# Softplus of dt made for two channel blocks at once in a fused Mamba and mixture-of-experts layer; six row buffers for expert tiles in place of seven

## The reference

```python
x = x + attn(_layernorm(x))     # the Mamba block, with a residual of its own
x = x + moe(_layernorm(x))      # top 2 of 8 experts

# the Mamba block, after its own layer norm
u, z = jnp.split(xn @ W_in.T, 2, axis=-1)                # 512 channels each
u_c = silu(causal_conv_4_taps(u) + conv_b)
dt, Bm, Cm = jnp.split(u_c @ W_xp.T, [16, 32], axis=-1)
dt = softplus(dt @ W_dt.T + b_dt)                        # per token and channel
h = exp(dt * A) * h + dt * u * B                         # 16 states per channel, over 1024 tokens
y = (h * C).sum(state) + u * D
out = x + (y * silu(z)) @ W_out.T

# the experts
weights, which = top_k(x @ router_w + router_b, 2); weights = softmax(weights)
out[token] += weight * ((silu(rows @ gate_e) * (rows @ up_e)) @ down_e)
```

## Time and profile before

| | |
|---|---|
| median of 3 runs | 2355.94 us (2353.19 to 2358.41) |
| span of the profiled execution | 2343.2 us, so 12.7 us of the median lie around the span |
| busy, share of the span | POOL 84%, DVE 81%, PE 77%, ACT 77% |
| granted TensorE clock, mean | 0.884 of 2.4 GHz |
| DMA engines, mean | 158 GB/s |

### The profile page before, as it was taken

How to read it: one execution, slowest core, us unless ns; L and a number is a source line. 1 busy time by engine, 2 the same in 40 slices (tenths; PEclk the granted TensorE clock), 3 DMA queues, 4 the chain that set the end, 5 groups by cost and what they waited for, 6 DMA issues and landing times.

```text
span 2343.2 us, 32677 instructions
## 1 busy us (share of the span) xinstructions
PE 1793.1 (77%) x7694; PEld 922.2 (39%) x7694; DVE 1891.2 (81%) x2437; ACT 1808.0 (77%) x3753; POOL 1961.7 (84%) x1320
## 2 busy tenths in 40 slices
...
GB/s 57 136 90 135 109 134 115 121 170 179 172 159 198 174 192 171 165 184 172 175 158 199 174 197 174 159 176 175 175 157 201 176 193 166 181 259 221 71 51 33
DMA packets 217980, 369.35 MB, mean 158 GB/s; under 512 B 31040, under 2 KB 86592, under 8 KB 217664
## 3 DMA queue, kind: packets, MB, share of 16 engines
...
...
## 4 chain that ended last, share of the span: by engine, by line
POOL 31%; issue 25%; PE 14%; ACT 12%; DVE 10%; DMA 7%; POOLq 1%; DVEq 0%; ACTq 0%; SPq 0%
POOL arena L1326 11%; DMA out<-yt,xt 6%; DVE dA L1114 5%; POOL arena L1334 5%; PE ring L605 4%; POOL sorted_x L1364 4%; POOL out L1374 3%; POOL rst L1290 3%; ACT dA L977 2%; DVE arena L1114 2%; POOL arena L1344 2%; POOL arena L1349 2%; PE yps L699 2%; PE ring L613 1%; PE ring L625 1%
## 5 line engine op out<-in xcount | busy, mean ns | idle before, releaser
L1326 POOL TENSOR_TENSOR arena<-arena,b_bc 128x2048 f32<-128x2048 f32 x256 | 998.6, 3901 | 64.8 <-PE yps L699 64.5
L977 ACT ACTIVATE dA<-arena,a_s 128x512 f32<-128x512 f32 x1024 | 680.7, 684 | 120.9 <-DVE arena L1123 74.7
L1114 DVE TENSOR_TENSOR_SCAN dA<-dA,arena 128x512 f32<-128x512 f32 x384 | 454.7, 1214 | 175.2 <-ACT dA L977 108.8
L1114 DVE TENSOR_TENSOR_SCAN dA<-dA,carry,arena 128x512 f32<-128x512 f32 x384 | 477.6, 1275 | 66.6 <-POOL arena L1326 49.8
L699 PE MATMUL yps<-arena,const_s 128*32 128x512 f32 x2048 | 321.3, 704 | 84.1 <-POOL arena L1334 53.6
L1334 POOL TENSOR_TENSOR arena<-arena,c_bc 128x511 f32<-128x511 f32 (+1 forms) x256 | 335.6, 1311 | 28.0 <-DVE arena L1114 26.4
L1123 DVE TENSOR_TENSOR arena<-dA,c_bc 128x1024 f32<-128x1024 f32 x256 | 313.6, 1225 | 8.8
L1374 POOL DMA_INDIRECT out<-yt,xt x135 | 214.7, 1590 | 116.5 <-ACT yt L1018 84.5
L597 PE MATMUL ring<-arena 128*128 128x512 f32 x488 | 271.7, 684 | 52.9 <-ACT arena L881 24.5
L731 PEld LDWEIGHTS p_g<-xT,w_e 128*128 128x128 f32 x1680 | 218.8, 211 | 125.4 <-issue 125.4
L605 PE MATMUL ring<-arena 128*128 128x512 f32 x480 | 235.3, 635 | 33.7 <-ACT arena L881 12.1
...
## 6 DMA issues: line engine op xcount, KB each, us to landing
arena<-dt_d SPq DMA_DIRECT2D x512, 256.0 KB
w_e<-in_w_moe SPq DMA_DIRECT2D x105, 512.0 KB, 4.7
dt_d<-arena SPq DMA_DIRECT2D x128, 256.0 KB, 2.4
w_e<-in_w_moe SPq DMA_DIRECT2D x105, 256.0 KB
...
b_bc<-bc_d SPq DMA_DIRECT2D x256, 64.0 KB, 2.4
c_bc<-bc_d SPq DMA_DIRECT2D x256, 64.0 KB, 3.5
...
```

The lines of the kernel that those rows point to most:

```text
L977: act.activation(dA[:, j, :], rep_dt[:, c % 2, j, :], ACT.Exp, scale=a_s[:, n, j:j + 1]).then_inc(s_exp, 1)
L1114: return dve.tensor_tensor_scan(out_ap, dA[:, j, :], hs[:, u % 3, j, :], init, ALU.mult, ALU.add)
L1326: pool.tensor_tensor(hs[:, u % 3], rep_dtu[:, c % 2], b_bc[:, g, :].unsqueeze(1).to_broadcast([P, J, T]), ALU.mult).then_inc(s_dbu, 1)
```

## The change

Blocks go in groups. Batch 0 has the groups (0), (1), (2, 3); every other batch (0, 1), (2, 3). `E` and `L` and POOL's four steps work on a whole group, 1024 wide for two blocks; `D` stays one block at a time. So the four POOL steps and the four ACT steps occur 33 times (3 + 15 x 2) in place of 64. Their slots, of a batch other than 0, in the kernel before and in this one:

| step | before, blocks 0, 1, 2, 3 | now, groups (0, 1), (2, 3) |
|---|---|---|
| `round_off` | -9, -4, -1, 1 | -9, -1 |
| `less_lost` | -8, -3, 0, 2 | -8, 0 |
| `plus_relu` | -7, -2, 0, 4 | -7, 1 |
| `dtu` | -6, -2, 0, 4 | -6, 2 |
| `store_dt` (SP) | -4, -1, 1, 6 | -5, -5, 3, 3 |

The tables for PE and ACT follow; the core of the diff:

```diff
-NX, NY = 7, 2
+NX, NY = 6, 2
 MAKES = {...
-         ["D0"], (-9, 1): ["Z0"], ... (-6, 0): ["D1"], (-2, 0): ["D2"], (0, 4): ["D3"]
+         ["D0"], (-9, 0): ["D1"], (-9, 2): ["Z0"], ... (-2, 0): ["D2"], (-1, 0): ["D3"]
 TAKES = {...
-         (-9, 0): ["D0", "E0"], (-9, 3): ["Z0"], (-8, 0): ["L0"], ...
-         (-6, 1): ["D1"], (-5, 1): ["E1"], (-3, 0): ["L1"], (-1, 0): ["D2", "E2"],
-         (0, 1): ["L2"], (1, 3): ["D3", "E3"], (2, 2): ["L3"]
+         (-9, 0): ["D0"], (-9, 2): ["D1", "E0"], (-9, 4): ["Z0"], (-8, 0): ["L0"], ...
+         (-1, 0): ["D2"], (-1, 1): ["D3", "E2"], (0, 1): ["L2"]
+def groups(q):
+    return ((0, 1), (1, 1), (2, 2)) if q == 0 else ((0, 2), (2, 2))
+def columns(q, k):
+    c, n = groups(q)[k]
+    return slice(c % 2, c % 2 + n)
-        t_s = sb("t_s", [P, T])
+        t_s = sb("t_s", [P, 2, T])
-        past = sb("past", [P, LAST, NE + 2])
-        full = sb("full", [P, NE, NTH])
+        past_t = sb("past", [P, NE + 2, LAST])          # full now lies in past's memory
             def exp_abs(q, c):
-                act.wait_ge(s_ract, TAKEN[q, f"D{c}"])
-                act.activation(dtub[:, c % 2, :], dtub[:, c % 2, :], ACT.Exp, scale=-1.0).then_inc(s_e, 1)
+                act.wait_ge(s_ract, TAKEN[q, f"D{sum(groups(q)[k]) - 1}"])
+                act.activation(dtub[:, of, :], dtub[:, of, :], ACT.Exp, scale=-1.0).then_inc(s_e, 1)
...
-            def round_off(q, c):
-                pool.wait_ge(s_s, CC * q + c + 1)
-                pool.tensor_tensor(t_s[:], t_s[:], dtub[:, c % 2, :], ALU.add).then_inc(s_t, 1)
+            def round_off(q, k):
+                pool.wait_ge(s_s, done_groups(q, k))
+                pool.tensor_tensor(t_s[:, of], t_s[:, of], dtub[:, of, :], ALU.add).then_inc(s_t, 1)
```

More of the change, by code:

```diff
@@ L131, in pieces, with group_at, group_of, done_groups @@
     return [(q, c) for q in range(NQ) for c in range(CC) if s == UN * q + (at if q > 0 else first)[c]]
+def groups(q):
+    return ((0, 1), (1, 1), (2, 2)) if q == 0 else ((0, 2), (2, 2))
+def group_at(s, at, first):
+    return [(q, k) for q in range(NQ) for k in range(len(groups(q))) if s == UN * q + (at if q > 0 else first)[k]]
+def group_of(q, c):
+    return next(k for k, (first, n) in enumerate(groups(q)) if first <= c < first + n)
+def done_groups(q, k):
+    return sum(len(groups(p)) for p in range(q)) + k + 1
+def columns(q, k):
+    c, n = groups(q)[k]
+    return slice(c % 2, c % 2 + n)
 def ahead(s, n, second):
@@ L277, in mamba_moe @@
         step = sb("step", [P, NE + 2])
-        past = sb("past", [P, LAST, NE + 2])
-        full = sb("full", [P, NE, NTH])
+        past_t = sb("past", [P, NE + 2, LAST])
+        past = past_t[:, :, :].rearrange("p e k -> p k e")
+        full = past_t[:, 0:NE - 2].rearrange("p e k -> p (e k)")[:, 0:NE * NTH].rearrange("p (e h) -> p e h", h=NTH)
         tef = sb("tef", [P, LAST])
@@ L541, in _ @@
                 front = 0 <= q + 1 < NQ
-                for p, k in pieces(s, (-4, -1, 1, 6), (-10, -1, 3, 6)):
+                for p, k in pieces(s, (-5, -5, 3, 3), (-10, -1, 3, 3)):
                     store_dt(p, k)
@@ L902, in exp_abs @@
             def exp_abs(q, c):
[L903 to L910 removed]
+                k = group_of(q, c)
+                of, v = columns(q, k), done_groups(q, k)
+                act.wait_ge(s_ract, TAKEN[q, f"D{sum(groups(q)[k]) - 1}"])
+                act.activation(dtub[:, of, :], dtub[:, of, :], ACT.Exp, scale=-1.0).then_inc(s_e, 1)
+                act.wait_ge(s_e, v)
+                wait(act, s_sub, v - 1)
+                act.activation(t_s[:, of], dtub[:, of, :], ACT.Identity, bias=1.0).then_inc(s_one, 1)
+                act.wait_ge(s_one, v)
+                act.activation(t_s[:, of], t_s[:, of], ACT.Identity, bias=1.0, scale=-1.0).then_inc(s_s, 1)
             def log_one(q, c):
[L913 to L914 removed]
+                k = group_of(q, c)
+                of = columns(q, k)
+                act.wait_ge(s_t, done_groups(q, k))
+                act.activation(dtub[:, of, :], dtub[:, of, :], ACT.Ln, bias=1.0).then_inc(s_l, 1)
             def silu_u(q):
```

44 lines of the change are left out of this document (19 added, 25 removed), and 14 rows, old and new, of tables (MAKES, MAKES0, TAKES, TAKES0).

## The result

The changed kernel takes 2515 us (median of four, 2502 to 2518) where the kernel before takes 2355 (2351 to 2358, measured beside it): ratio 1.068, 95% interval 1.064 to 1.071. The forecast was 2461 with a range of 2385 to 2500: the direction was right, the size was not.

The account below looks back on a forecast made before the run. The prediction took POOL to set the pace in slots 7 to 11: 3.8 + 3.8 - 0.6 = 7.0 us a batch, slots 12 to 6 at 0. 15 x 7.0 = 105 on 2356 gave 2461 us, range 2385 to 2500.

Parts of the forecast that it names:

- Bound of slots 7 to 11: Slots 7 to 11: POOL is the tight engine, each microsecond put into it moves every later scan; loss 7.0 us a batch.
- parts 1 and 2: Slots 7 to 11: `round_off` waits 3.8 us for ACT's t; wider POOL pieces add 3.8, a wait for `place` saves 0.6.
- prices: POOL's 1024-wide pieces take 2.00 us, wide `plus_relu` 1.1 more than its 1.28; ACT's 1024 columns take 1.06.
- POOL sets the pace: Slots 7 to 11: POOL has 35.7 us with one 0.61 wait, while DVE sits idle 5.71 for the `drive` of unit 12.
- Part 3: Slots 7 and 8: `K0`, `place` and first scatter some 3 us later, no extra cost as POOL comes later still; floor 5.9.
- Part 4: Slots 12 to 6: POOL's and ACT's shifts net to 0 us a batch, bounds -5.1 to +2.
- 2.2 - 1.4 + 1.3: POOL's lateness: `drive` of unit 1 2.2 us later, slot 0 1.4 less work, slot 1 1.3 more.
- ACT's 6.4 us less in slots 1 and 2: ACT loses a take, three steps and a logarithm with its loads, which can shorten DVE's 3.37 wait at unit 6.
- Parts at nothing: Joined stores, block 2's reads, six `xt` buffers, the tail's loads and `full` in `past`'s memory: no cost.
- more is lost: Rival: POOL's delay in slots 15 to 3 isn't made up, or the tail waits for loads: 2491 and more; chance 0.08.
- The saving pays: Rival: 80 us of ACT's table loads and 22 us of POOL's fixed parts go: 2305 or 2334; chance 0.13.
- The lead is given back: Rival: slots 12 to 6 return 3 to 5 of the 7.0, through ACT's 6.4 us: 2386 to 2416; chance 0.15.

Follow-up runs that it names:

- e18: Kernel before with only ACT's work for block 1 moved up to slot 7 and `D1` ahead of `Z0`, all pieces 512 wide: 2425 us, ratio 1.031.
- e11: Changed kernel with the first pair's `round_off` one slot later, `less_lost` beside `plus_relu`: 2557 us, ratio 1.086.
- e12: Changed kernel with both edits, `K0` ahead of `Z0` and the first pair's `round_off` one slot later: 2513 us, ratio 1.068.
- e10: Changed kernel with `K0` put ahead of `Z0` in the ring: 2510 us, ratio 1.068.
- e15: Changed kernel with only blocks 0 and 1 paired; ACT's block 3 work in slot 15, POOL's pieces for blocks 2, 3 512 wide in old slots: 2450 us, 1.042.
- e14: Kernel before with only ACT's work and matmul for block 3 moved up to slot 15, all pieces 512 wide: 2397 us, ratio 1.018.
- e20: Changed kernel with the stores of blocks 1 and 3 in the slots of the kernel before: 2521 us, ratio 1.071.
- e1: Kernel before with six row buffers and nothing else: 2353 us, ratio 0.999.

## Why the prediction was wrong

**Bound of slots 7 to 11, parts 1 and 2, prices: right, one reason incomplete.** The forecast was 7.0 us a batch, measured 6.9. `round_off` waits 3.3 to 3.9 in slot 7 (3.8 forecast), the wide pieces take 2.00 and 2.35, the logarithm's loads are 33. But the two terms are not one wait and four longer pieces: ACT's joined block, with `D1` ahead of `Z0`, makes 4.4 (e18) and the wide pieces the other 2.5. So that the sum came out at 6.9 is in part luck. e11 and e12 show that the wait is not `round_off`'s own; it goes to whatever POOL wants next from ACT, directly or through DVE's `place`. "POOL sets the pace" was half of it: POOL and ACT set it together. DVE's wait at unit 12 came out at 7.6 in the mean (7.7 to 8.3 in most batches, 5.4 before) and not at 9 or more: of the stretch's 6.9 only 2.2 are that wait; DVE was busy for 3.8 more, 3.1 of that in one small instruction (last section), and waited 1.0 more at units 8 and 11. In e12 that instruction is short again, DVE waits at units 10 to 12 instead, and the stretch is as long.

**Part 3: right in direction.** I put `K0` 3 us later and hidden behind POOL. It is 4.3 to 4.5 later (medians of even and odd batches, 5.1 in batch 8) and about ties with POOL. That it costs nothing while `round_off` waits holds (e10), and that it takes the place of that wait holds too (e11: 4.19).

**Part 4: the step that failed.** It read "I take 0, since the two work on the same stretch in turn", with bounds from -5.1 to +2; measured is +4.6 (12 to 15: -0.6, 0 to 3: +2.9, 4 to 6: +2.2), above the upper bound. Two errors are in it. First, I netted POOL's lateness in slots 15 to 2 against its earliness from slot 4 on, "+0.6 by slot 5, with a peak of 3 at the drive of unit 4, where DVE waits already now". Its first term was right: `round_off` of slot 15 went 1.2 later (1.3 forecast). But the drive of unit 3 ended 3.2 later after unit 15's product than before (mean of 14 batches; by my terms 2.2 - 1.4 + 1.3 = 2.1), since I missed POOL's wait for the landing of an add, 2.77 in slot 1 of batch 8 and 1.7 in the mean. DVE's scan of unit 3 moved by the same 3.2 (4.84 of waiting for 1.09). The waits that DVE had at units 2 and 3 didn't cover it, because ACT's joined block had used them up: it had made DVE 2.4 late at unit 1 already. And being early later is worth nothing: POOL just waits longer for PE (120.3 us for 64.5, in slot 6 6.0 a batch for 2.3). Second, ACT's 6.4 us less in slots 1 and 2 was to shorten DVE's wait at unit 6; it did not: DVE's 2.00 for the exponential and 2.35 for the tanh are together more than the 3.37 before, and ACT's own waits for PE grew (130.5 us for the gate products). e15 places the loss: with block 3's takes and exponential joined on ACT, but POOL's pieces and the logarithms apart, it is not there.

The 2.2 in slots 4 to 6 go with PE's granted clock. By batch (2 to 14) the stretch from unit 4 to unit 7 takes 27.6 to 27.7 us at 1.00 and 28.4 to 29.4 at 0.94 in the kernel before, and 31.8 at 0.84 in two batches of e14; in the changed kernel 28.5 at 0.94, 30.3 to 30.8 at 0.87 to 0.89, 30.4 to 32.0 at 0.84 and 0.85, 32.6 to 33.7 at 0.80 and below. At a like clock it is about as long without the change as with it, but the mean clock there fell from 0.96 to 0.85. What lowered it no run shows, and the clock isn't all of it: e20 takes 1.0 longer than e15 at the same 0.94. The stretch in batch 8 of the kernel before (us, busy us of PE, PEld, DVE, ACT and POOL with counts, granted clock, DMA share, GB/s):

```profile
1154.33:1183.64 29.31, 25.46 (x111) 11.47 (x110) 25.49 (x39) 24.41 (x52) 23.74 (x15) 0.94 0.74 162
```

the same stretch in the changed kernel:

```profile
1236.46:1267.78 31.32, 28.03 (x106) 13.61 (x105) 25.70 (x40) 23.12 (x50) 22.29 (x14) 0.85 0.75 170
```

the same stretch in e20:

```profile
1240.90:1271.22 30.32, 24.93 (x106) 11.61 (x104) 25.49 (x40) 23.85 (x52) 23.08 (x14) 0.94 0.77 191
```

and in e15:

```profile
1206.16:1235.46 29.30, 24.60 (x103) 11.31 (x102) 25.48 (x39) 24.39 (x52) 23.70 (x15) 0.94 0.74 163
```

**Parts at nothing: right as far as shown.** Six buffers cost nothing (e1). From the last unit's product to the end the trace has 180.4 us, before 180.0. Of the stores, the `drive` of unit 0 now waits 1.6 us in the mean for block 0's load, but DVE starts unit 0 no later after unit 15's product than before (3.5 us, before 3.8); whether the joint store costs anything in slots 0 to 6 stays open (e20).

**Rivals.** The one that came is "more is lost", given 0.08: "POOL's delay in slots 15 to 3 isn't made up, +2 to +3 a batch more"; it was 4.6. "The saving pays" failed as argued, and the Trainium skill's rule in "ScalarE: Activation LUTs", section "Table sets: the hidden batching unit" (all activations of one set before switching), did remove the loads here, 62 of them, without a gain: ACT's time was not what the batch lacked, its order was. "The lead is given back" has the sign wrong.
